# Turning h by DMA instead of by TensorE in a fused cross-attention and expert kernel

## The chip, the cores and the metric

The kernel runs on one core of a Trainium2 chip. The metric is the device time of one execution in microseconds. The kernel before took 281.07 us (median of three runs, 281.0 to 282.23). All times in the text are microseconds.

## The reference, cut to what matters

`x` is 4 x 512 x 512 (2048 rows of 512), float32. Two stages follow each other:

```
h   = layernorm(x)                                   # per row
e   = expert of the row's token id                   # 4 experts, ctx[e] is 512 x 512
out = (silu(h @ ctx[e].T) * (h @ ctx[e].T)) @ ctx[e].T   # down projection by the same matrix
x1  = x + tanh(g_xattn) * out
h2  = layernorm(x1); per batch: gate on mean(h2), the best 2 of 6 experts
y   = sum of the two experts' gelu(h2 @ W1 + b1) @ W2 + b2, weighted
res = x1 + tanh(g_ffn) * y
```

In the first stage the gate and the up projection are one product, so a tile takes two products of 512 x 512.

## The kernel before, in words

The rows are sorted by expert into 19 tiles of 128 rows (`TILES`), padded where an expert's rows end. A tile j goes through this: GpSimd (POOL) gathers its rows from `x` by an indirect DMA into one of 7 places of `x_ring` (`gather`, L502); VectorE (DVE) takes mean and variance (`rows_statistics`, L661); POOL raises variance + eps to the power -1/2 (`inverse_root`, L506); DVE writes the normalised rows into the one buffer `h` (`normalise`, L683); TensorE (PE) turns `h` by four 128 x 128 transposes (`transpose_h`, L1189); ScalarE (ACT) rounds the turned tile into `hT_hi` (`h_high`, L960) and DVE takes the rest as `hT_lo` (`h_low`, L689). PE then makes the first product from twelve matmuls of 512 columns (hi x hi, hi x lo, lo x hi: `first_product`, L1235). ACT takes silu (`silu_of`), DVE multiplies (`up`, L702) into the one buffer `a`, PE turns `a` (`transpose_a`, L1196), ACT rounds it (`a_high`, L965), DVE takes the rest (`a_low`, L696), and PE makes the second product, twelve matmuls again. DVE adds it to the rows in the ring (`add`, L668) and takes their statistics (`statistics`, L673). POOL raises that variance too and scatters the rows to DRAM by an indirect DMA (`scatter`, L511); `landed(j)` (L518) waits until this scatter has landed, after which a gather may overwrite that place of the ring.

The work of each engine is written out by hand, in order, and each engine runs its list in order; semaphores stand between them. In step j of the steady part (j from 5) PE does `transpose_a(j-1)`, `transpose_h(j+1)`, `first_product(j)`, `second_product(j-1)`. DVE does `add(j-2)` and `a_low(j-1)` (in either order), `rows_statistics(j+2)`, `statistics(j-2)`, `up(j)`, `normalise(j+2)`, `h_low(j+1)`. ACT does `a_high(j-1)`, `silu_of(j)`, `h_high(j+1)`. POOL's loop over j (L555) does `inverse_root(j+4)`, `scatter(j)`, `landed(j-1)`, `gather(j+6)`; so its turn j falls into PE's step j+2. Steps 12 to 18 (`PREP` on) carry work for the second stage besides: DVE normalises `x1` of the first batch in steps 12 and 13, PE turns it in step 14 (`transpose_first_h2`), ACT rounds it there (`ffn_h_high(0)`, L1019), and PE makes the gate's logits at the head of step 15 (`logits`, L1346), which wait for that rounding; ACT's `exponents(0)` with two table loads follows in step 15. SyncE (SP) loads `x1` of the first batch once seven tiles have landed, and the experts' weights once the gate has chosen.

In the second stage a batch has a first half (s = 0) and a second (s = 1), each with three blocks of hidden columns, gelu, and output. Weights are parted into hi (`split_high`, ACT, L1051) and lo (`split_low`, `split_low_last`, DVE). For batches 2 and 3 (`by_dma`, L188) the turn of `h2` is already done by DMA: ACT parts each float32 into two 16-bit words (`part_words`, L1029), SP issues `dma_start_transpose` (`turn_words`, L450), ACT joins the words again (`join_words`, L1038).

Of the kernel before, what the change touches and what calls it, by code (L numbers as in the profile page):

```python
# [33 lines left out]
P = 128  # L34
# [41 lines left out]
def flamingo_kernel(nc, x, ids, ctx, g_xattn, g_ffn, gate_w, w1, b1, w2, b2, out):  # L76
# [19 lines left out]
    PAIRED = range(E + 1, TILES)  # L96
    LATER = TILES - E
    BY_ACT = (0, 1)
    BY_DVE = tuple(n for n in range(E * KD) if n not in BY_ACT)
# [18 lines left out]
    with ExitStack() as stack:  # L118
# [15 lines left out]
        h = sb("h", [P, D])  # L134
        hT_hi = sb("hT_hi", [P, KD, P], FP32R)
        hT_lo = sb("hT_lo", [P, KD, P], FP32R)
        a = sb("a", [P, F1])
# [29 lines left out]
        hT1_lo = nc.alloc_sbuf_tensor_at("hT1_lo", [P, KD, P], FP32R, offset=w_lo1 + KD * P * 4)  # L167

        def hT_of(j):
            return (hT1_hi, hT1_lo) if j == 1 else (hT_hi, hT_lo)  # L170

# [177 lines left out]
        b1_padded, masks_made = sem("b1_padded"), sem("masks_made")  # L349
        half_copied, folded = sem("half_copied"), sem("folded")  # L350
        words_made, words_joined = sem("words_made"), sem("words_joined")
        words_turned = [sem(f"words_turned{t}") for t in range(TT)]
# [35 lines left out]
        def _(sp):  # L388
# [51 lines left out]
            def store(b):  # L440
                for t in range(TT):
                    store_rows(sp, b, t, halves_of(b, t)[0], TT * b + t + 1)

            sp.wait_ge(ctxT_done, E * KD)
            sp.wait_ge(tiles_landed, EARLY)
            load_x1(0)
            sp.wait_ge(rows_done, 1)
            sp.wait_ge(pads_made, 2)
# [27 lines left out]
        def _(pool):  # L476
# [77 lines left out]
            gather(E + 2, E + 2)  # L554
            for j in range(1, TILES):  # L555
                paired = j + 2 in PAIRED or j + 3 in PAIRED
                if paired and j + AHEAD < TILES:
                    inverse_root(j + AHEAD)
                scatter(j, j % RING)
                if not paired and j + AHEAD < TILES:  # L560
                    inverse_root(j + AHEAD)
                landed(j - 1)
                if j + RING - 1 < TILES:
                    gather(j + RING - 1, (j - 1) % RING)
            landed(TILES - 1)


        @block.vector
        def _(dve):
# [113 lines left out]
            def normalise(j):  # L683
                dve.wait_ge(rstd_ready, j + 1)
                at_least(dve, hT_done, j)
                dve.tensor_scalar(h[:, :], ring_row(j, 0, D), mv1[:, 0:1], rstd1[:, :],
                                  ALU.subtract, ALU.mult).then_inc(h_ready, 1)

            def h_low(j):  # L689
                dve.wait_ge(hT_hi_done, j + 1)  # L690
                hi, lo = hT_of(j)
                dve.tensor_tensor(lo[:, :, :].rearrange("p k t -> p (k t)"), hT_bank(j)[:, :],
                                  hi[:, :, :].rearrange("p k t -> p (k t)").bitcast(FP32),
                                  ALU.subtract).then_inc(hT_lo_done, 1)
# [57 lines left out]
            rows_of(slice(E, TILES), o_ps[0], LATER, routed)  # L752
            ctx_low(15)
            for j in range(2, PREP):
                a_low(j - 1)
                if j in PAIRED or j + 1 in PAIRED:
                    if j not in PAIRED:
                        normalise(j + 1)
                    add(j - 2, y_ps)
                    rows_statistics(j + 2)  # L760
                    statistics(j - 2)
                    up(j)
                    normalise(j + 2)
                    h_low(j + 1)
                else:
                    if j > 2:
                        normalise(j + 1)
                        residual(j - 2)
                    h_low(j + 1)
                    up(j)  # L770
                    rows_statistics(j + 2)
# [44 lines left out]
            def split_low(b, s, piece):  # L816
                dve.wait_ge(hi_done[s], len(PARTS) * b + piece + 1)
                raw, hi, lo = w_raw[s], w_hi[s], w_lo[s]
                if s == 0 or piece == 0:
                    dve.tensor_tensor(part_of(lo, piece), part_of(raw, piece), part_of(hi, piece).bitcast(FP32),  # L820
                                      ALU.subtract).then_inc(lo_done[s], 1)
                elif piece == 1:

                    dve.tensor_tensor(rest_of(hi, P + LW, REST), rest_of(raw, P, P + LW), rest_of(hi, P, P + LW).bitcast(FP32),
                                      ALU.subtract)
                    dve.tensor_tensor(rest_of(lo, 0, P), rest_of(raw, 0, P), rest_of(hi, 0, P).bitcast(FP32),
                                      ALU.subtract).then_inc(lo_done[s], 1)
                else:
                    dve.tensor_tensor(lo[:, W1N:WN - D], raw[:, W1N:WN - D], hi[:, W1N:WN - D].bitcast(FP32),  # L829
                                      ALU.subtract).then_inc(lo_done[s], 1)  # L830
# [51 lines left out]
            for j in range(PREP, TILES):  # L882
                if j == PREP + 3:
                    scale_logits(0)
                add(j - 2, y_ps)
                a_low(j - 1)
                if j + 2 < TILES:
                    rows_statistics(j + 2)
                statistics(j - 2)
                up(j)  # L890
                if j + 2 < TILES:
                    normalise(j + 2)
                if j + 1 < TILES:
                    h_low(j + 1)
                if j < PREP + 2:
# [18 lines left out]

            def batch(b, more):
                weigh(b, 0, 0)
                weigh(b, 0, 1)
                split_low(b, 1, 0)
                split_low(b, 1, 1)
                weigh(b, 0, 2)  # L920
                if more and not by_dma(b + 1):
                    ffn_normalise(b + 1)
                if not by_dma(b + 1):
                    split_low_last(b)
                if more:
# [3 lines left out]
                    mixing(b + 1)  # L929
                if by_dma(b + 1):  # L930
                    split_low_last(b)
                split_low(b, 1, 2)
                weigh(b, 1, 0)
# [20 lines left out]
        def _(sc):  # L954
# [58 lines left out]
            for n in range(12, 16):  # L1013
                ctx_high(n)
            for j in range(2, PREP):
                a_high(j - 1)
                silu_of(j)
                h_high(j + 1)
            def ffn_h_high(b, banks):  # L1019
# [61 lines left out]
            for j in range(PREP, TILES):  # L1081
                a_high(j - 1)
                if j == TILES - 1:
                    split_high(0, 0, 2)
                silu_of(j)
                if j + 1 < TILES:
                    h_high(j + 1)
                if j == PREP + 2:
                    ffn_h_high(0, o_ps)
                if j == PREP + 3:  # L1090
                    exponents(0)
                    bring_tables(ACT.Silu)
                if j == PREP + 5:
                    split_high(0, 0, 0)
                    split_high(0, 0, 1)
# [4 lines left out]
            def batch(b, more):  # L1100

                bring_tables(ACT.Gelu)
                wait_apart(sc, gate_ready, b + 1, waited)
                chosen = [sc.value_load(top_idx[0:1, s:s + 1], min_val=0, max_val=NE - 1) for s in range(2)]
                gelu_of(b, 0, 0, chosen)
                split_high(b, 1, 0)
                split_high(b, 1, 1)
                if by_dma(b + 1):
                    join_words(b + 1, [0])
                gelu_of(b, 0, 1, chosen)  # L1110
                if by_dma(b + 1):
                    join_words(b + 1, [1, 2])
                else:
                    split_high(b, 1, 2)
                for c in range(2, FC):
                    gelu_of(b, 0, c, chosen)
                if by_dma(b + 1):
                    join_words(b + 1, [3])
                    sc.wait_ge(words_joined, TT * b)
                if more:  # L1120
                    ffn_h_high(b + 1, t_ps)
                    if by_dma(b + 1):
                        split_high(b, 1, 2)
                    bring_tables(ACT.Exp)
# [20 lines left out]
        def _(pe):  # L1145
# [164 lines left out]
            def tile_step(j):  # L1310
# [3 lines left out]
                transpose_a(j - 1)  # L1314
                if j in PAIRED:
                    transpose_h(j + 1)
# [29 lines left out]
            def logits(b):  # L1346
                if isinstance(b, int) and b == 0:
                    pe.wait_ge(h2T_hi_done, KD)
                    pe.wait_ge(hT_lo_done, PREP + 4)
                else:  # L1350
# [68 lines left out]
            for j in range(PREP, TILES):  # L1419
                if j == PREP + 3:  # L1420
                    logits(0)
                transpose_a(j - 1)
                if j == PREP + 3:
                    pe.wait_ge(neg_max_ready, 1)
                if j + 1 < TILES:
                    transpose_h(j + 1)
                first_product(j, e)
# [61 lines left out]
```

## Time and profile before

| | |
|---|---|
| runs | 281.07 median, 281.0 to 282.23 |
| the profiled execution, its own time | 281.05 |
| its span, first to last instruction | 279.2 |
| PE busy, share of the span | 97% |
| DVE, ACT, POOL busy | 77%, 48%, 25% |
| granted TensorE clock | full speed in all 40 slices |

The span is about 1.9 us shorter than the execution's own time; what lies around it is start and end of the program. The shares of busy time are averages over both stages. The row stage (19 tiles) lasts until about 142 us, the expert stage from there to the end. "L1211" is the line of `product` and stands for the row stage's matmuls; L1193 are the turns of `h`, L1202 those of `a`.

### The profile page before, as it was taken

The page shows a single profiled execution, that of the slowest core. Times are in us where ns is not written, and L with a number is a line of the kernel's source. Part 1 is how long each engine was busy: PE and PEld are TensorE (multiplying, and loading weights), DVE is VectorE, ACT ScalarE, POOL GpSimd, SP SyncE. Part 2 cuts the span into 40 slices and gives each one's busy share as a digit, 9 for nine tenths or more (in the row PEclk, how much of TensorE's full clock was granted, in tenths as well). Part 3 has the DMA queues.
Part 4 walks back from the last instruction along what each step waited for, and adds up shares of the span by engine and source line. Part 5 has one row for each costly group of instructions (what it writes and reads, how often), then busy time and mean ns, then how long its engine had stood idle before and what let it go on. Part 6 is the DMA issues. An engine that isn't in the chain of part 4 may idle for free.

```text
span 279.2 us, 4519 instructions
## 1 busy us (share of the span) xinstructions
PE 271.9 (97%) x1400; PEld 222.3 (80%) x1400; DVE 215.7 (77%) x500; ACT 133.7 (48%) x216; POOL 70.1 (25%) x113
## 2 busy tenths in 40 slices
PE   7999999999999999999999999999999999999995
PEld 6888888888888888888788877878768777788783
DVE  8798988877777888688996769975799649878074
ACT  4745322222222223462627185799576994634020
POOL 5565165555544555324133000000000000000000
PEclk9999999999999999999999999999999999999999
DMA  6870033222356322319702637994299504940004
GB/s 196 299 249 14 2 112 113 79 75 86 106 104 210 102 77 78 75 40 280 230 38 78 195 108 224 257 256 151 53 300 209 176 2 117 307 163 2 0 0 150
DMA packets 32610, 37.10 MB, mean 133 GB/s; under 512 B 12584, under 2 KB 21038, under 8 KB 32588
## 3 DMA queue, kind: packets, MB, share of 16 engines
q1 hardware_dynamic: 29376, 26.69, 32.8%
q0 software_dynamic: 3040, 9.98, 12.0%
q8 instruction: 12, 0.20, 0.3%
q10 hardware_dynamic: 172, 0.15, 0.2%
q14 instruction: 10, 0.08, 0.1%
HBM read 25.52 MB, written 9.19 MB: 124 GB/s over the span
## 4 chain that ended last, share of the span: by engine, by line
PE 75%; ACT 10%; DVE 7%; issue 3%; DMA 2%; POOL 0%; ACTq 0%; SPq 0%; DVEq 0%
PE bank L1211 38%; PE bank L1185 8%; PE bank L1187 8%; PE bank L1186 8%; PE bank L1193 3%; PE bank L1202 3%; ACT joined L1043 3%; DMA raw_ctx<-in_ctx 2%; ACT w_hi L1058 2%; PE bank L1263 2%; ACT ctx_hi L1026 1%; PE bank L1408 1%; PE bank L1409 1%; DVE x_even L879 1%; DVE w_lo L829 1%
## 5 line engine op out<-in xcount | busy, mean ns | idle before, releaser
L1185 PE MATMUL bank<-w_lo,ctx_hi 128*128 128x512 f32 x80 | 31.8, 397 | 0.1
L1187 PE MATMUL bank<-w_hi,ctx_lo 128*128 128x512 f32 x80 | 31.2, 391 | 0.0
L1186 PE MATMUL bank<-w_hi,ctx_hi 128*128 128x512 f32 x80 | 31.2, 390 | 0.0
L973 ACT ACTIVATE a<-bank 128x512 f32<-128x512 f32 x19 | 11.4, 599 | 40.5 <-PE bank L1211 40.5
L968 ACT ACTIVATE aT_hi<-bank 128x512 fp32r<-128x512 f32 x18 | 10.8, 598 | 33.9 <-PE bank L1202 33.9
L1058 ACT ACTIVATE w_hi<-w_raw 128x512 fp32r<-128x512 f32 (+3 forms) x24 | 23.7, 1019 | 1.4 <-DMA w_raw<-in_L_ffn_W 1.4
L1185 PE MATMUL bank<-ctx_lo,w_hi 128*128 128x512 f32 x60 | 23.6, 394 | 0.0
L1211 PE MATMUL bank<-ctx_hi,hT_hi 128*128 (+1 forms) x80 | 23.3, 414 | 0.1
L1186 PE MATMUL bank<-ctx_hi,w_hi 128*128 128x512 f32 x60 | 23.4, 390 | 0.0
L1187 PE MATMUL bank<-ctx_hi,w_lo 128*128 128x512 f32 x60 | 23.4, 390 | 0.0
L503 POOL DMA_INDIRECT x_ring<-in_x,get_rows x19 | 19.3, 1016 | 14.8 <-DVE put_rows L653 9.8
L1065 ACT ACTIVATE act<-bank,tables 128x512 f32<-128x512 f32 x16 | 11.0, 685 | 24.6 <-PE bank L1187 24.1
L1211 PE MATMUL bank<-ctx_hi,hT_lo 128*128 (+1 forms) x80 | 21.6, 392 | 0.0
L1211 PE MATMUL bank<-ctx_lo,hT_hi 128*128 (+1 forms) x80 | 21.5, 391 | 0.0
L515 POOL DMA_INDIRECT x_scratch<-x_ring,put_rows x19 | 20.1, 1056 | 5.4 <-POOL x_ring L514 5.4
L698 DVE TENSOR_TENSOR aT_lo<-bank,aT_hi 128x512 fp32r<-128x512 f32 x18 | 12.4, 688 | 10.4 <-ACT aT_hi L968 10.3
L1211 PE MATMUL bank<-ctx_hi,aT_hi 128*128 (+1 forms) x72 | 19.9, 398 | 0.0
L508 POOL TENSOR_TENSOR rstd<-ve,half 128x1 f32<-128x1 f32 x19 | 10.8, 571 | 36.1 <-DVE ve L666 36.1
L1211 PE MATMUL bank<-ctx_hi,aT_lo 128*128 (+1 forms) x72 | 19.6, 392 | 0.0
L1211 PE MATMUL bank<-ctx_lo,aT_hi 128*128 (+1 forms) x72 | 19.3, 390 | 0.0
L870 DVE TENSOR_SCALAR ctx_hi<-act,mix 128x512 fp32r<-128x512 f32 x16 | 7.7, 483 | 13.7 <-ACT act L1065 13.6
L1185 PEld LDWEIGHTS bank<-w_lo,ctx_hi 128*128 128x128 f32 x80 | 15.0, 188 | 4.0 <-issue 0.9
(221 smaller groups left out, 625.6 us busy)
## 6 DMA issues: line engine op xcount, KB each, us to landing
raw_ctx<-in_ctx SPq DMA_DIRECT2D x4, 1024.0 KB, 8.1
w_raw<-in_L_ffn_W SPq DMA_DIRECT2D x8, 512.0 KB, 4.9
x_even<-x_scratch SPq DMA_DIRECT2D x8, 257.0 KB, 3.8
w_raw<-in_L_ffn_W SPq DMA_DIRECT2D x8, 256.0 KB, 4.6
w_raw<-in_L_ffn_W SPq DMA_DIRECT2D x4, 448.0 KB, 3.6
out<-x_even SPq DMA_DIRECT2D x7, 256.0 KB, 2.4
w_raw<-in_L_ffn_W SPq DMA_DIRECT2D x4, 384.0 KB, 6.4
x_odd<-x_scratch SPq DMA_DIRECT2D x4, 257.0 KB, 3.4
```

The source lines that it names most:

```text
L503: pool.indirect_dma_start(x_ring[:, r * DS:r * DS + D], None, x_rows, bass.IndirectOffsetOnAxis(get_rows[:, j:j + 1], 0)).then_inc(gathere ...
L508: pool.tensor_tensor(rstd1[:, :], ve1[:, :], half[:, 0:1], ALU.pow).then_inc(rstd_ready, 1)
L515: pool.indirect_dma_start(x1_rows, bass.IndirectOffsetOnAxis(put_rows[:, j:j + 1], 0), x_ring[:, r * DS:(r + 1) * DS], None).then_inc(scat ...
L698: dve.tensor_tensor(lo[:, :, :].rearrange("p k t -> p (k t)"), bank[:, :], hi[:, :, :].rearrange("p k t -> p (k t)").bitcast(FP32), ALU.su ...
L968: sc.activation(aT_hi[:, :, :].rearrange("p k t -> p (k t)"), aT_ps[:, :], ACT.Copy).then_inc(aT_hi_done, 1)
L973: sc.activation(a[:, :], z_bank(j)[:, :], ACT.Silu).then_inc(silu_done, 1)
L1058: sc.activation(part_of(w_hi[s], piece, s), part_of(w_raw[s], piece, s), ACT.Copy).then_inc(hi_done[s], 1)
L1065: sc.activation(act[:, c % 2, :], hid_ps[k % 2][:, :], ACT.Gelu, bias=b1_of(s, c, slice(0, P), chosen[s])).then_inc(gelu_done, 1)
L1185: pe.matmul(dst, s_hi, m_lo, start=first, stop=False)
L1186: pe.matmul(dst, s_hi, m_hi, start=False, stop=False)
L1187: return pe.matmul(dst, s_lo, m_hi, start=False, stop=last)
L1211: return pe.matmul(dst[:, :], src[:, k, :], weights[:, bass.ds(e * (KD * F1) + k * F1, F1)], start=first, stop=last)
```

## The change

For tiles 7 to 18 (`TURNED` = 7) the turn of `h` leaves PE. After `normalise`, ACT parts `h` into 16-bit words (`part_row`), SP turns the 128 x 1024 words by one DMA transpose (`turn_row_words`), and ACT joins them (`join_row`) and rounds the joined tile into `hT_hi`; DVE's `h_low` reads the joined tile. Tiles of odd number get buffers of their own. In these steps `rows_statistics` and `normalise` run three tiles ahead instead of two, `normalise` waits until ACT has parted the tile before, and stands ahead of `up` in DVE's list; POOL's loop has from its third turn on the order `landed`, `gather`, `inverse_root`, `scatter`. SP's load of the first batch's `x1` stands behind the DMA transposes of tiles 7 to 13. In batches 1 and 2 of the expert stage the last piece of the second half's weights is split before the first gelu, and the joins are placed later. The diff, cut to its core:

```diff
@@ -166,8 +168,17 @@
+        row_words = nc.alloc_sbuf_tensor_at("row_words", [P, 2, 2, D], U16, offset=weights + 3 * WN * 4)
+        row_words_T = nc.alloc_sbuf_tensor_at("row_words_T", [P, 2, 2 * KD, P], U16, offset=weights + 3 * WN * 4 + 8 * D)
+        hT_joined = [nc.alloc_sbuf_tensor_at("hT_joined0", [P, KD * P], FP32, offset=hT_lo_at),
+                     nc.alloc_sbuf_tensor_at("hT_joined1", [P, KD * P], FP32, offset=w_lo1 + KD * P * 4)]
+        def turned(j):
+            return TURNED <= j < TILES
         def hT_of(j):
-            return (hT1_hi, hT1_lo) if j == 1 else (hT_hi, hT_lo)
+            return (hT1_hi, hT1_lo) if j == 1 or (turned(j) and j % 2) else (hT_hi, hT_lo)
...
@@ -441,9 +454,18 @@
+            def turn_row_words(js):
+                for j in js:
+                    sp.wait_ge(row_words_made, j - TURNED + 1)
+                    sp.dma_start_transpose(row_words_T[:, j % 2], row_words[:, j % 2].rearrange("p g d -> p (g d)")).then_inc(
+                        row_words_turned[j % 2], 16)
             sp.wait_ge(ctxT_done, E * KD)
+            turn_row_words(range(TURNED, EARLY + TURNED))
             sp.wait_ge(tiles_landed, EARLY)
             load_x1(0)
+            turn_row_words(range(EARLY + TURNED, TILES))
             sp.wait_ge(rows_done, 1)
...
@@ -552,16 +574,26 @@
             gather(E + 2, E + 2)
-            for j in range(1, TILES):
+            for j in range(1, TURNED - AHEAD):
                 paired = j + 2 in PAIRED or j + 3 in PAIRED
-                if paired and j + AHEAD < TILES:
+                if paired:
                     inverse_root(j + AHEAD)
                 scatter(j, j % RING)
-                if not paired and j + AHEAD < TILES:
+                if not paired:
                     inverse_root(j + AHEAD)
+                landed(j - 1)
+                gather(j + RING - 1, (j - 1) % RING)
+            for j in range(TURNED - AHEAD, TILES):
                 landed(j - 1)
                     gather(j + RING - 1, (j - 1) % RING)
+                if j == TURNED - AHEAD:
+                    inverse_root(j + AHEAD)
+                if j > TURNED - AHEAD and j + AHEAD + 1 < TILES:
+                    inverse_root(j + AHEAD + 1)
+                scatter(j, j % RING)
+                if j == TURNED - AHEAD:
+                    inverse_root(j + AHEAD + 1)
             landed(TILES - 1)
...
@@ -682,14 +714,16 @@
                 dve.wait_ge(rstd_ready, j + 1)
-                at_least(dve, hT_done, j)
+                at_least(dve, hT_done, min(j, TURNED))
+                at_least(dve, row_words_made, j - TURNED)
                 dve.tensor_scalar(h[:, :], ring_row(j, 0, D), mv1[:, 0:1], rstd1[:, :],
                 hi, lo = hT_of(j)
-                dve.tensor_tensor(lo[:, :, :].rearrange("p k t -> p (k t)"), hT_bank(j)[:, :],
+                source = hT_joined[j % 2] if turned(j) else hT_bank(j)
+                dve.tensor_tensor(lo[:, :, :].rearrange("p k t -> p (k t)"), source[:, :],
                                   hi[:, :, :].rearrange("p k t -> p (k t)").bitcast(FP32),
...
@@ -751,7 +785,23 @@
             ctx_low(15)
+            def row_step(j):
+                add(j - 2, y_ps)
+                a_low(j - 1)
+                if j + 3 < TILES:
+                    rows_statistics(j + 3)
+                statistics(j - 2)
+                if j + 3 < TILES:
+                    normalise(j + 3)
+                up(j)
+                if j + 1 < TILES:
+                    h_low(j + 1)
             for j in range(2, PREP):
+                if j >= TURNED - 1:
+                    row_step(j)
+                    continue
                 a_low(j - 1)
...
@@ -762,6 +812,9 @@
                     h_low(j + 1)
+                    if j == TURNED - 2:
+                        rows_statistics(j + 3)
+                        normalise(j + 3)
                 else:
...
@@ -882,16 +936,7 @@
                     scale_logits(0)
-                add(j - 2, y_ps)
-                a_low(j - 1)
-                if j + 2 < TILES:
-                    rows_statistics(j + 2)
-                statistics(j - 2)
-                up(j)
-                if j + 2 < TILES:
-                    normalise(j + 2)
-                if j + 1 < TILES:
-                    h_low(j + 1)
+                row_step(j)
                 if j < PREP + 2:
...
@@ -913,23 +958,27 @@
             def batch(b, more):
+                joined_ahead = by_dma(b + 1)
                 weigh(b, 0, 0)
                 split_low(b, 1, 1)
+                if joined_ahead:
+                    split_low_last(b)
                 weigh(b, 0, 2)
-                if more and not by_dma(b + 1):
-                    ffn_normalise(b + 1)
-                if not by_dma(b + 1):
+                if joined_ahead:
+                    split_low(b, 1, 2)
+                else:
+                    if more:
+                        ffn_normalise(b + 1)
                     split_low_last(b)
                     mixing(b + 1)
-                if by_dma(b + 1):
-                    split_low_last(b)
-                split_low(b, 1, 2)
+                if not joined_ahead:
+                    split_low(b, 1, 2)
                 weigh(b, 1, 0)
...
@@ -1012,10 +1061,37 @@
                 ctx_high(n)
+            def part_row(j):
+                sc.wait_ge(h_ready, j + 1)
+                at_least(sc, row_words_turned[j % 2], 16 * ((j - TURNED) // 2))
+                sc.activation(row_words[:, j % 2], h[:, :].bitcast(U16).rearrange("p (d g) -> p g d", g=2),
+                              ACT.Copy).then_inc(row_words_made, 1)
+            def join_row(j):
+                sc.wait_ge(row_words_turned[j % 2], 16 * ((j - TURNED) // 2 + 1))
+                sc.wait_ge(z_done, j - 1)
+                to = hT_joined[j % 2][:, :].bitcast(U16).rearrange("p (k s g) -> p g k s", k=KD, g=2)
+                sc.activation(to, row_words_T[:, j % 2].rearrange("p (g k) s -> p g k s", g=2), ACT.Copy).then_inc(row_words_joined, 1)
+                sc.wait_ge(row_words_joined, j - TURNED + 1)
+                sc.activation(hT_of(j)[0][:, :, :].rearrange("p k t -> p (k t)"), hT_joined[j % 2][:, :], ACT.Copy).then_inc(hT_hi_done, 1)
+            def tile_step(j):
+                a_high(j - 1)
+                if turned(j + 1):
+                    join_row(j + 1)
+                silu_of(j)
+                if j + 1 < TURNED:
+                    h_high(j + 1)
+                if j == TURNED - 2:
+                    part_row(TURNED)
+                if j >= TURNED - 2 and turned(j + 3):
+                    part_row(j + 3)
             for j in range(2, PREP):
-                a_high(j - 1)
-                silu_of(j)
-                h_high(j + 1)
+                tile_step(j)
             def ffn_h_high(b, banks):
...
@@ -1102,25 +1178,23 @@
                 chosen = [sc.value_load(top_idx[0:1, s:s + 1], min_val=0, max_val=NE - 1) for s in range(2)]
+                joined_ahead = by_dma(b + 1)
+                if joined_ahead:
+                    split_high(b, 1, 2)
                 gelu_of(b, 0, 0, chosen)
                 split_high(b, 1, 1)
-                if by_dma(b + 1):
-                    join_words(b + 1, [0])
                 gelu_of(b, 0, 1, chosen)
-                if by_dma(b + 1):
-                    join_words(b + 1, [1, 2])
+                if joined_ahead:
+                    join_words(b + 1, [0, 1])
                 else:
                     split_high(b, 1, 2)
-                for c in range(2, FC):
-                    gelu_of(b, 0, c, chosen)
-                if by_dma(b + 1):
-                    join_words(b + 1, [3])
+                gelu_of(b, 0, 2, chosen)
+                if joined_ahead:
+                    join_words(b + 1, [2, 3])
                     sc.wait_ge(words_joined, TT * b)
                     ffn_h_high(b + 1, t_ps)
-                    if by_dma(b + 1):
-                        split_high(b, 1, 2)
                     bring_tables(ACT.Exp)
...
@@ -1312,7 +1386,7 @@
                 transpose_a(j - 1)
-                if j in PAIRED:
+                if j in PAIRED and not turned(j + 1):
                     transpose_h(j + 1)
...
@@ -1346,7 +1420,7 @@
                     pe.wait_ge(h2T_hi_done, KD)
-                    pe.wait_ge(hT_lo_done, PREP + 4)
+                    pe.wait_ge(hT_lo_done, TURNED)
                 else:
...
@@ -1420,10 +1494,6 @@
                 transpose_a(j - 1)
-                if j == PREP + 3:
-                    pe.wait_ge(neg_max_ready, 1)
-                if j + 1 < TILES:
-                    transpose_h(j + 1)
                 first_product(j, e)
```

## Rows read from the trace of the kernel before

**Rows 1.** The page, part 1: busy us (share of the span) xinstructions of each engine.

```profile
PE 271.9 (97%) x1400; PEld 222.3 (80%) x1400; DVE 215.7 (77%) x500; ACT 133.7 (48%) x216; POOL 70.1 (25%) x113
```

**Rows 2.** Chain that ended last, in order of time: start us, us, what.

```profile
62.67 0.44 PE bank L1202 x4
...
88.07 0.44 PE bank L1202 x4
...
88.51 0.44 PE bank L1193 x4
...
107.13 0.44 PE bank L1202 x4
...
115.53 0.59 PE bank L1202 x4
...
135.01 0.44 PE bank L1202 x4
```

**Rows 3.** DVE, instructions in order of time: start, us, operation, idle before.

```profile
54.88 0.54 DVE L686 TENSOR_SCALAR h<-x_ring,mv,rstd 128x512 f32<-128x512 f32 x1
...
89.17 0.69 DVE L698 TENSOR_TENSOR aT_lo<-bank,aT_hi 128x512 fp32r<-128x512 f32 x1 [1.31 <-ACT aT_hi L968]
...
92.46 0.68 DVE L704 TENSOR_TENSOR a<-bank,a 128x512 f32<-128x512 f32 x1
...
93.51 0.68 DVE L692 TENSOR_TENSOR hT_lo<-bank,hT_hi 128x512 fp32r<-128x512 f32 x1
```

**Rows 4.** ACT, instructions in order of time, same columns.

```profile
88.54 0.60 ACT L968 ACTIVATE aT_hi<-bank 128x512 fp32r<-128x512 f32 x1 [2.08 <-PE bank L1202]
...
91.74 0.60 ACT L973 ACTIVATE a<-bank 128x512 f32<-128x512 f32 x1 [2.60 <-PE bank L1211]
...
120.52 1.28 ACT L1048 ACT_TABLE_LOAD   x1
...
123.51 0.20 ACT L979 ACTIVATE warm<-tg 1x2 f32<-1x2 f32 x1
```

**Rows 5.** POOL, instructions in order of time, same columns.

```profile
91.61 0.57 POOL L508 TENSOR_TENSOR rstd<-ve,half 128x1 f32<-128x1 f32 x1 [2.15 <-DVE ve L666]
...
92.62 0.55 POOL L514 TENSOR_TENSOR x_ring<-x_ring,half 128x1 f32<-128x1 f32 x1 [0.44 <-DVE x_ring L677]
...
93.46 1.07 POOL L515 DMA_INDIRECT x_scratch<-x_ring,put_rows  x1 [0.29 <-POOL x_ring L514]
...
94.83 0.97 POOL L503 DMA_INDIRECT x_ring<-in_x,get_rows  x1 [0.30 <-issue]
```

**Rows 6.** Scatters (L515), landing of all, of 55 to 108 us, of 140 to 148 us.

```profile
DMA to landing us min/median/max: 2.8/3.7/6.5
...
DMA to landing us min/median/max: 3.1/3.9/5.3
...
DMA to landing us min/median/max: 3.4/3.5/3.5
```

**Rows 7.** DMA transposes (L454), landing of all eight, us from issue.

```profile
DMA to landing us min/median/max: 3.1/4.1/5.6
```

**Rows 8.** Groups of instructions by form: xcount, busy us, mean ns.

```profile
L1043 ACT ACTIVATE joined<-words_T 128x1024 uint16<-128x1024 uint16 x8 | 10.6, 1362 | 0.0
...
L1035 ACT ACTIVATE words<-h 128x1024 uint16<-128x1024 uint16 x8 | 8.0, 1041 | 0.0
...
L1026 ACT ACTIVATE h2T_hi<-bank 128x512 fp32r<-128x512 f32 x4 | 2.3, 615 | 0.0
```

**Rows 9.** PE and ACT in the expert stage, in order of time.

```profile
207.18 0.47 PE L1408 MATMUL bank<-w_hi,ctx_hi 128*128 128x512 f32 x1 [0.49 <-DVE ctx_hi L858]
...
181.91 0.69 ACT L1065 ACTIVATE act<-bank,tables 128x512 f32<-128x512 f32 x1 [1.86 <-PE bank L1187]
...
193.34 0.63 ACT L1057 ACTIVATE w_lo<-b_rows 64x512 fp32r<-64x512 f32 x1
...
193.98 1.49 ACT L1058 ACTIVATE w_hi<-w_raw 128x1536 fp32r<-128x1536 f32 x1
```

More of the change, by code:

```diff
@@ L97, in flamingo_kernel @@
     LATER = TILES - E
+    TURNED = E + 3
     BY_ACT = (0, 1)
@@ L135, in flamingo_kernel @@
         hT_hi = sb("hT_hi", [P, KD, P], FP32R)
+        hT_lo_at = (nc.sbuf_base + 31) // 32 * 32
         hT_lo = sb("hT_lo", [P, KD, P], FP32R)
@@ L350, in flamingo_kernel @@
         half_copied, folded = sem("half_copied"), sem("folded")
+        row_words_made, row_words_joined = sem("row_words_made"), sem("row_words_joined")
+        row_words_turned = [sem(f"row_words_turned{i}") for i in range(2)]
         words_made, words_joined = sem("words_made"), sem("words_joined")
@@ L816, in split_low @@
             def split_low(b, s, piece):
-                dve.wait_ge(hi_done[s], len(PARTS) * b + piece + 1)
+                place = (1, 2, 0)[piece] if s == 1 and by_dma(b + 1) else piece
+                dve.wait_ge(hi_done[s], len(PARTS) * b + place + 1)
                 raw, hi, lo = w_raw[s], w_hi[s], w_lo[s]
@@ L1081, in _ @@
             for j in range(PREP, TILES):
-                a_high(j - 1)
                 if j == TILES - 1:
+                    a_high(j - 1)
                     split_high(0, 0, 2)
-                silu_of(j)
-                if j + 1 < TILES:
-                    h_high(j + 1)
+                    silu_of(j)
+                else:
+                    tile_step(j)
                 if j == PREP + 2:
@@ L1422, in _ @@
                 transpose_a(j - 1)
-                if j == PREP + 3:
-                    pe.wait_ge(neg_max_ready, 1)
-                if j + 1 < TILES:
-                    transpose_h(j + 1)
                 first_product(j, e)
```

## The prediction

> **What bounds the kernel now.** I read the page's busy shares first: PE 97%, DVE 77%, ACT 48%, POOL 25% [rows 1]. Then the chain that ended last, in order of time. In the row stage it is PE alone: a turn of a (0.44), a turn of h (0.44), 24 matmuls, and again. I call S_j the start of `transpose_a(j-1)` in step j. From S_11 = 88.07 to S_14 = 107.13 a step takes 6.35 [rows 2]. The timelines of the other engines inside one step show who could follow a faster PE. DVE works from 89.17 to 94.19, 5.0 of the 6.35, and sat idle before for 1.31 [rows 3]. ACT rounds a at S+0.47 and makes silu at S+3.67 [rows 4]; it has two thirds of the step free. POOL has its root, its power for the scatter, the scatter, the gather [rows 5], and nothing in the step before waits for it. So PE bounds the row stage, and turns of h taken from PE are worth 0.44 each if all others keep pace: 12 x 0.44 = 5.3. A step would be 5.91.
>
> **POOL's new order (the deciding term).** Before, turn j of POOL's loop is root, scatter(j), then `landed(j-1)`, whose scatter was issued a whole step earlier, then gather: no wait. After, it is `landed(j-1)`, gather(j+6), root(j+5), scatter(j). Now the scatter that POOL waits for is the one it issued last, and the root that DVE needs in this very step stands behind it. Behind the root wait `normalise(j+3)` and, in DVE's list, `up(j)`, and so PE's next turn of a. This is a ring within POOL. Its length, from end of root to end of root: power 0.55, gap 0.29, scatter issued to landed L, gap 0.30, gather 0.97, root 0.57 [rows 5], and twice 0.05 that I estimate between its instructions: 2.78 + L. L isn't on a row of the new order. Bounds: 2.8, the lowest of all 19, and 3.9, the median of the nine steady ones, which have a gather issued close behind [rows 6]; below by nothing more, above 5.3, one that met the load of x1. I take 3.45, from the two scatters with no indirect transfer behind them (3.4 and 3.5): in the new order the next gather is issued only after the landing, and the last one has its packets out before. The ring is then 6.23, against PE's 5.91 and 6.35 before. DVE isn't the limit: its 5.0 of work has the same instructions in another order.
>
> The Trainium skill, page "DMA: Bandwidth & Descriptors", section "Anatomy of one DMA — SWDGE (gpsimd) path", puts a DMA issued by GpSimd at about 2.0 plus its bytes over 436 GB/s. For 263 KB that is an estimate of 2.6, below each of the 19 landings here, and the ring would be 5.4, shorter than PE's step. The page adds that the receipt of a write to HBM can be slow, and a scatter writes to HBM. Its formula is the first rival below; the sum doesn't use it.
>
> **The way in (tiles 7 and 8).** `normalise(7)` ends at 55.42 [rows 3]. `part_row` costs 1.04 [rows 8], the DMA transpose 4.1 (3.1 to 5.6) [rows 7]: landed at 60.7. The join 1.36 [rows 8], rounding 0.60, silu(6) 0.60 behind it in ACT's list, `up(6)` 0.68: PE can begin step 7 at 64.1 instead of 62.67 [rows 2]. At the same time POOL's root(8) stands behind scatter(3), ends at 57.7 and lets `normalise(8)` end at 58.3, `part_row(8)` at 59.4; `a_high(5)` is queued behind it and ends at 60.0. From there a_low 0.65, two statistics 2 x 1.05: 62.75; power, gap, scatter issued at 63.65, landed 67.1, gap, gather, root: POOL's root in step 7 ends at N_7 = 69.0. From a root's end to PE's next step I count 0.08, normalise 0.45 (start to next start), up 0.68 and 0.06 = 1.27. S_8 = 70.3.
>
> **Steps 8 to 15.** Seven turns of the ring: N_14 = 69.0 + 7 x 6.23 = 112.6. Step 14 brings `ffn_h_high(0)`, which now stands behind `part_row(17)` in ACT's list, and that waits for `normalise(17)`: 112.6 + 0.62 + 1.1 = 114.3, then four roundings, 2.3 [rows 8], 116.7; the logits, which wait for them, 0.28: S_15 = 117.0 against 115.53 [rows 2], 1.5 late.
>
> **Steps 15 to 18.** POOL's turns have no gather now and are off the path. ACT in step 15: `normalise(18)` ends at S+4.3, part_row at S+5.35, the exponents with two table loads 3.2 (120.52 to 123.71 [rows 4]), `a_high(15)` at S+9.2, join and rounding 2.06, silu 0.6, up 0.7: S_17 = S_15 + 12.65 where PE alone gives 11.82. S_18 = S_15 + 18.55 = 135.55. Before it was 135.01. The row stage is **0.55 longer**: the 5.3 of removed turns are paid back by 1.5 on the way in, by the ring (7 x 0.32), by the logits' wait and by ACT's exponents. The gate's choice comes some 2 later, which the weights' loads can bear, as their split stands behind silu(17).
>
> **What costs nothing.** SP's DMA transposes: from `part_row(j+3)` to `join_row(j+3)` lie over 6, the landing is 4.1, at most 5.6 [rows 7]; if that cover went, each microsecond over would delay silu. Moving x1's load behind them: it lands about 97, wanted at 100; behind it nothing on SP is due before the gate. `h_low` from SBUF instead of PSUM: the same 0.68.
>
> **The expert stage's order.** Before, PE waits 0.49 for a DVE result at 207.18, and once more a batch later [rows 9]. The moved splits free DVE earlier, so both can go: -1.0. But ACT's split of the second half's last piece (0.63 + 1.49) now stands ahead of the first gelu, at 181.91 before [rows 9]. It needs weights and bias rows whose issue ended at 176.5; by the landings of the DMA transposes of the same stretch [rows 7] they are there at 179.6 to 182.1. ACT is free at 180.1, so the gelu comes at 182.2 to 184.3. PE's third hidden block asks for it at 184.3, its end 0.66 later: 0 to 0.6 lost, and the second gelu with its weighing, behind two more splits, 0 to 0.9. For two batches -1.0 to +0.8. I take +0.3, nearer the late end, since these rows are queued last behind the weights.
>
> **Sum.** 281.05 (the profiled execution's own time: span 279.2 and 1.9 around it) + 0.55 + 0.3 = 281.9; the median of the runs, 281.07, is the same. By 0.5%, 1.4, a measurement can tell this kernel from no change: 281.9 lies 0.3% above.
>
> **Rivals.**
> 1. *The ring is short.* If L is 2.8, as in one scatter of 19, the ring is 5.58 and PE's 5.91 binds. S_14 = 70.3 + 6 x 5.91 = 105.75, S_15 = that + 8.40 - 0.44 = 113.7, S_18 = 132.25, 2.75 earlier; with 0.3: **278.6**. It counts as faster from a ring of 5.91, L = 3.13; some steady scatters were at 3.1 [rows 6]. That the median of these is 3.9 speaks against.
> 2. *The ring is long.* One mechanism on the slow side: the landing of the scatter with a DMA transpose and a gather about it. At L = 3.9 the ring is 6.68, 7 x 0.45 = 3.15 more: **285.1**. It decides from L = 3.53 on (0.08 per turn). For it: a DMA transpose per step is new traffic. Against: by my times its packets come after the scatter's.
> 3. *All is hidden,* way in included: -5.3 and -1.0, **274.8**. Needs POOL and ACT both off the path.
> 4. *The change doesn't do what it says in the expert stage:* the row stage as forecast, but the early split costs its full 0.8: 282.4.
>
> **Chances.** Forecast (279.7 to 283.3) with rival 4: 0.45; rival 1: 0.24; rival 2: 0.26; rival 3: 0.05. Of the forecast's 0.45 about 0.31 lies within 0.5%, 0.12 above, 0.02 below. Faster 0.31, same 0.31, slower 0.38. The likeliest case's own range is 280.2 to 283.3; the range from rival 1 to rival 2 with the expert stage's bounds is 277.8 to 285.1.
>
> **What would show it.** Steps 8 to 14 of PE at 6.2, not 5.9, with PE idle before L1202 for DVE's a; `normalise` (L686's successor) waiting for POOL's root; POOL waiting for landings of its own scatters, near 3.45. S_7 at 64.1. PE waiting before the logits. Steps of 5.9 throughout would prove the ring wrong; steps over 6.5 rival 2. In the expert stage the waits at L1408 gone, and new ones of under 1 before the third hidden block and the first output of batches 1 and 2. Wrong altogether if DVE, not POOL, is what `up` waits behind.

## The result: 5% slower

The changed kernel took 295.19 (median of four runs, 293.75 to 297.27); the kernel before, beside it, 281.5 (281.0 to 282.23). The ratio is 1.0495, 95% interval 1.0466 to 1.0524. The forecast was 281.9, at most 285.1. The profiled execution of the changed kernel is its slowest run, 297.27, with a span of 295.5. Ratios in this text are taken over runs within 1.5% of the fastest of their kernel, which leaves out two of the ten runs of the last experiment and none of the others.

The page of the kernel after, part 1 (busy us and share of the span), the row of granted clock in 40 slices, and two groups of part 5:

```profile
PE 274.5 (93%) x1352; PEld 220.6 (75%) x1352; DVE 217.1 (73%) x500; ACT 162.9 (55%) x240; POOL 73.3 (25%) x113
...
PEclk9999999999979999979999979999999999999999
...
L525 POOL DMA_INDIRECT x_ring<-in_x,get_rows x19 | 18.8, 991 | 44.9 <-DMA x_scratch<-x_ring,put_rows 33.4
...
L719 DVE TENSOR_SCALAR h<-x_ring,mv,rstd 128x512 f32<-128x512 f32 x19 | 10.5, 551 | 15.2 <-POOL rstd L530 14.9
```

PE's share fell from 97% [rows 1] to 93%, with 48 turns fewer. POOL is busy 25% as before, yet its gathers now wait 33.4 for landings of scatters, and DVE's `normalise` waits 14.9 for POOL's root. A low busy share didn't mean that POOL was off the path.

The chain that ended last, in order of time, kernel after, three turns of POOL's ring (start us, us, what):

```profile
71.80 4.88 DMA x_scratch<-x_ring,put_rows
76.72 0.77 issue
77.49 0.98 POOL x_ring L525
78.48 0.58 POOL rstd L530
79.06 0.63 POOL x_ring L536
79.69 0.28 issue
79.96 3.65 DMA x_scratch<-x_ring,put_rows
83.65 0.77 issue
84.42 0.98 POOL x_ring L525
85.41 0.59 POOL rstd L530
86.00 0.62 POOL x_ring L536
86.62 0.28 issue
86.90 3.52 DMA x_scratch<-x_ring,put_rows
...
120.24 0.59 POOL rstd L530
```

Where the chain of before is PE alone [rows 2], this one has no PE from 63 to 121. It is scatter, landing, gather, root, power, scatter. In the timeline of PE (start, busy, operation, idle before), the heads of two steps of the kernel after:

```profile
72.14 0.66 PE L1276 MATMUL bank<-ident,a 128*128 128x128 f32 x4 [2.14 <-DVE a L738]
80.30 0.66 PE L1276 MATMUL bank<-ident,a 128*128 128x128 f32 x4 [2.04 <-DVE a L738]
```

Later in the same chain, the end of the row stage's scatters and the load of the second batch's rows:

```profile
138.23 7.63 DMA x_scratch<-x_ring,put_rows
...
148.09 3.16 DMA x_scratch<-x_ring,put_rows
...
161.90 3.98 DMA x_scratch<-x_ring,put_rows
...
167.29 5.00 DMA x_odd<-x_scratch
172.32 0.56 DVE h L831
172.93 1.33 PE bank L1407 x8
```

Starts of PE's steps, from the chains and timelines of PE, and the difference:

| | before | after | later by | eight places in the ring (below) |
|---|---|---|---|---|
| step 7 | 62.67 | 63.88 | 1.2 | 63.77 |
| step 14 | 107.13 | 115.22 | 8.1 | 105.30 |
| step 15 | 115.53 | 125.13 | 9.6 | 113.50 |
| step 18 | 135.01 | 144.72 | 9.7 | 132.14 |
| logits of the second batch | 164.38 | 179.18 | 14.8 | 161.69 |
| logits of the fourth batch | 228.57 | 245.57 | 17.0 | 225.69 |
| span | 279.2 | 295.5 | 16.3 | 275.6 |

8.1 comes by step 14, 1.5 with the logits' wait in step 14, 0.1 in steps 15 to 17, 5.1 with the second batch's rows, 2.2 in batches 1 and 2, and 0.7 comes back behind them. In steps 15 to 17 three removed turns should have gained 1.3; why they didn't is told below, at the granted clock.

### The profile page after: what moved, and what is told of

It reads as the page before. It is cut to its first block, busy times and chain, and to the rows that moved or that the text cites. A ratio compares the mean times of both kernels' runs of the same rounds, so it can differ in the third digit from the quotient of the medians.

```text
span 295.5 us, 4457 instructions
## 1 busy us (share of the span) xinstructions
PE 274.5 (93%) x1352; PEld 220.6 (75%) x1352; DVE 217.1 (73%) x500; ACT 162.9 (55%) x240; POOL 73.3 (25%) x113
## 4 chain that ended last, share of the span: by engine, by line
PE 39%; DMA 25%; POOL 8%; issue 7%; ACT 7%; DVE 6%; SPq 6%; ACTq 0%; DVEq 0%; POOLq 0%
DMA x_scratch<-x_ring,put_rows 19%; PE bank L1285 9%; PE bank L1259 7%; PE bank L1261 6%; PE bank L1260 6%; DMA b_rows<-in_L_ffn_b 4%; POOL x_ring L536 3%; POOL x_ring L525 3%; PE bank L1337 3%; POOL rstd L530 2%; ACT w_hi L1134 2%; DMA x_odd<-x_scratch 2%; PE bank L1227 1%; SPq L451 1%; PE bank L1276 1%
## 5 line engine op out<-in xcount | busy, mean ns | idle before, releaser
L525 POOL DMA_INDIRECT x_ring<-in_x,get_rows x19 | 18.8, 991 | 44.9 <-DMA x_scratch<-x_ring,put_rows 33.4
L1068 ACT ACTIVATE row_words<-h 128x1024 uint16<-128x1024 uint16 x12 | 12.7, 1057 | 21.7 <-DVE h L719 21.7
L1285 PE MATMUL bank<-ctx_hi,hT_hi 128*128 (+1 forms) x80 | 24.2, 426 | 0.3 <-ACT hT_hi L1012 0.3
L1285 PE MATMUL bank<-ctx_lo,hT_hi 128*128 (+1 forms) x80 | 23.3, 415 | 0.0
L537 POOL DMA_INDIRECT x_scratch<-x_ring,put_rows x19 | 21.4, 1127 | 5.4 <-POOL x_ring L536 5.4
L1285 PE MATMUL bank<-ctx_hi,hT_lo 128*128 (+1 forms) x80 | 22.5, 404 | 0.0
L719 DVE TENSOR_SCALAR h<-x_ring,mv,rstd 128x512 f32<-128x512 f32 x19 | 10.5, 551 | 15.2 <-POOL rstd L530 14.9
L874 DVE TENSOR_TENSOR w_lo<-w_raw,w_hi 128x512 fp32r<-128x512 f32 (+2 forms) x16 | 17.1, 1086 | 3.2 <-ACT w_hi L1134 3.1
```

Of the source, the lines that this page charges most:

```text
L525: pool.indirect_dma_start(x_ring[:, r * DS:r * DS + D], None, x_rows, bass.IndirectOffsetOnAxis(get_rows[:, j:j + 1], 0)).then_inc(gathere ...
L537: pool.indirect_dma_start(x1_rows, bass.IndirectOffsetOnAxis(put_rows[:, j:j + 1], 0), x_ring[:, r * DS:(r + 1) * DS], None).then_inc(scat ...
L1068: sc.activation(row_words[:, j % 2], h[:, :].bitcast(U16).rearrange("p (d g) -> p g d", g=2), ACT.Copy).then_inc(row_words_made, 1)
L1285: return pe.matmul(dst[:, :], src[:, k, :], weights[:, bass.ds(e * (KD * F1) + k * F1, F1)], start=first, stop=last)
```

## The experiments

Theory A: POOL's ring (its wait for the scatter that it issued last) sets the step, and the same order makes the last scatters a file that delays the second batch's rows. Rival B: the DMA transposes' traffic slows every landing. Rival C: ACT's parting and joining stand in the way. Rival D came later: that what a larger ring gains has nothing to do with the turns taken from PE.

### Eight places in the ring

```diff
-    RING = 7
+    RING = 8
 ...
-                landed(j - 1)
-                if j + RING - 1 < TILES:
-                    gather(j + RING - 1, (j - 1) % RING)
+                landed(j - 2)
+                if j + RING - 2 < TILES:
+                    gather(j + RING - 2, (j - 2) % RING)
```

The eighth place lies in memory that the expert stage uses later; the edit also has POOL wait for the turned `ctx`, and ACT for the landings, before either side uses that memory.

> The kernel after with one more place in the ring of rows (8 instead of 7, the eighth in memory that the expert stage uses later): gather(j+6) and the wait in front of it now stand for scatter(j-2), issued a whole step earlier, instead of scatter(j-1). Everything else is the kernel after: DMA transposes, three tiles ahead, POOL's order, the expert stage's order. Theory A (POOL's wait for its own last scatter sets the step, and what follows from it downstream): no wait of POOL's gathers for a landing in steps 8 to 14, PE's step 5.9 to 6.0 instead of about 7.2, step 15 begins near 114 instead of 125, and the whole takes 278 to 282. Rival B (the DMA transposes' traffic, some 12,700 more packets, slows the landings and with them everything): the step stays above 6.6 and the time above 288. Rival C (ACT's parting and joining stand too long ahead of silu and the rounding of a): steps above 6.3 with PE waiting for ACT, 284 to 290.

Measured: 277.87 (277.35 to 278.49), ratio to before 0.9884, interval 0.9861 to 0.9908. The turns of DMA and the order of DVE, ACT and POOL are those of the kernel after; only the wait is for a landing one step older. PE's steps in its timeline:

```profile
69.76 0.60 PE L1287 MATMUL bank<-ident,a 128*128 128x128 f32 x4
75.69 0.60 PE L1287 MATMUL bank<-ident,a 128*128 128x128 f32 x4
```

5.93 a step, without idle time before. Its waits (us in total, times, longest), and the landings of its scatters from 55 to 120 us:

```profile
POOL x_ring L531 <- DMA x_scratch<-x_ring,put_rows: 0.9, 1, 0.9
...
DVE h L728 <- POOL rstd L536: 0.7, 1, 0.7
```

```profile
DMA to landing us min/median/max: 4.9/5.1/5.3
```

Of the 33.4 that POOL's gathers waited, 0.9 is left. Rival B had a true part: landings are longer here than before, 5.1 against 4.0 in the same stretch, with a DMA transpose and a gather about each. But a landing that nobody waits for costs nothing. C and B fall as causes of the 5%: against the kernel after, 17.3 are gone, 9.9 of them by step 14.

### POOL's order alone, in the kernel before

```diff
-            for j in range(1, TILES):
+            for j in range(1, 3):
 ...
+            for j in range(3, TILES):
                 landed(j - 1)
                 if j + RING - 1 < TILES:
                     gather(j + RING - 1, (j - 1) % RING)
+                if j + AHEAD < TILES:
+                    inverse_root(j + AHEAD)
+                scatter(j, j % RING)
```

> The kernel before with one edit: POOL's loop has from its third turn on the order landed(j-1), gather(j+6), inverse_root(j+4), scatter(j). TensorE turns h as before, two tiles ahead, no DMA transposes. Theory A: POOL's ring of power, scatter, landing, gather and root comes to about 6.7 to 7.0 against PE's 6.35; the root that normalise(j+2) waits for comes late, steps grow by 0.3 to 0.6, and the load of the second batch's rows behind the last landing comes late besides: 284 to 290. Rival B: without DMA transposes the order costs nothing, 281 to 282.

Measured: 289.5 (287.92 to 291.2), ratio 1.0272, interval 1.0235 to 1.0308. No DMA transpose runs in its row stage, and the chain shows the same ring:

```profile
90.12 0.58 POOL rstd L508
90.70 0.62 POOL x_ring L514
91.60 4.76 DMA x_scratch<-x_ring,put_rows
96.41 0.77 issue
97.17 0.97 POOL x_ring L503
98.17 0.58 POOL rstd L508
```

From the root's end at 63.03 to that at 105.74 are six turns, 7.1 each. The kernel after has (120.83 - 70.90) / 7 = 7.1. The landings in these turns are 3.8 on the mean here and 3.85 there. The ring has the same length with and without DMA transposes: B is refuted for the ring.

### The same order with eight places

The last kernel with the ring's edit of the first experiment on top.

> The kernel before with POOL's new order and eight places in the ring: TensorE turns h, two tiles ahead, but POOL's wait is for a scatter issued a step earlier. Against the kernel with POOL's order alone (289.5) only the ring differs. Theory A: POOL is off the path again, PE's step is 6.35, and the time is that of the kernel before, 280.5 to 282. If the eight places gained anything by themselves (rival D: the gain of the kernel with DMA transposes and eight places comes from the ring and not from the turns taken from PE), it would be below 280, near 278.

Measured: 280.95 (280.7 to 281.77), ratio 0.9999, interval 0.9989 to 1.001. The order costs 8.5 with seven places and nothing with eight. The larger ring gains nothing of itself (rival D falls), so the gain of the first experiment against before comes with the rest of the change.

### The tail

```diff
             for j in range(TURNED - AHEAD, TILES):
-                landed(j - 1)
+                if j < TILES - 5:
+                    landed(j - 1)
 ...
                 scatter(j, j % RING)
+                if j >= TILES - 5:
+                    landed(j - 1)
```

> The kernel after with one edit: in POOL's turns 14 to 18, which gather nothing, scatter(j) stands before landed(j-1) again. The ring of turns 3 to 13 stays, so step 15 begins at 125 as in the kernel after. What goes is the file of scatters that wait for one another; the second batch's rows are then loaded at about 159 instead of 166, before PE wants them turned, and its wait of 3.3 with the stretch at half the clock behind it is gone. Theory A with its two parts (ring, then late load): 289 to 292 against 295.2. Rival: the load is bound by something else, no change (294 to 296).

Measured: 289.13 (286.97 to 290.21), ratio to before 1.0309, interval 1.0286 to 1.0333, 6.1 less than the kernel after. All five runs lie below all four of the kernel after. PE's wait of 3.28 before the second batch's turns isn't in its trace. The ring is left as it was, yet in the profiled execution, the fastest (286.97), step 15 begins at 122.6 and not at 125.1, and step 18 at 141.2 and not at 144.7: single landings and the granted clock vary between two executions. The other 6.8 by which the two spans differ come behind step 18. So the medians' 6.1 is the price of the tail only as nearly as such variation lets one say. The one order cost in two places: of the 17.3 between seven and eight places 9.9 stand at step 14, and about 6 come through its last five turns.

### The expert stage's order by itself, twice

The edit is the change's part in batches 1 and 2, put into the kernel before, and taken out of the kernel with eight places.

> The kernel before with only the new order of the expert stage in batches 1 and 2 (early split of the second half's last piece, later joins). In the kernel after, PE waits there 0.85 and 0.33 per batch before the third hidden block and the first output, where before it waited 0.49 and 0.2 per batch. So 0.5 to 1.2 slower than before: 281.6 to 282.3. The forecast had put -1.0 to +0.8 on it. If instead the waits in the kernel after come only from its late row stage, this kernel is 0.5 to 1.0 faster than before.

Measured: 281.0 (ten runs, 279.52 to 282.04), ratio 0.9992, interval 0.9973 to 1.0011. No difference in the runs, so neither of the two expectations.

> The kernel with eight places in the ring, with the expert stage's order of the kernel before. Row stage as in that kernel; if the expert order costs 0.5 to 1.2, this one is that much faster than it: 277 to 281. If it is the slower of the two, the new expert order is a gain once the row stage is in time.

Measured: 279.11 (278.91 to 279.58), ratio to before 0.9927, interval 0.9909 to 0.9945; with the new order 277.87. Here the new order is worth 1.2 and no loss. In the kernel after, PE did wait for it, as the forecast had it for a late split (timeline of PE, batch 1):

```profile
200.19 0.50 PE L1259 MATMUL bank<-ctx_lo,w_hi 128*128 128x512 f32 x1 [0.85 <-ACT act L1141]
...
203.53 0.47 PE L1259 MATMUL bank<-w_lo,ctx_hi 128*128 128x512 f32 x1 [0.33 <-DVE ctx_lo L925]
```

With eight places only the second of these is left (0.35 and 0.28 in the two batches); with the kernel before's row stage both are there, 0.17 and 0.33 in batch 1. The traces show more than the medians. From the start of the second batch's logits to the end of the span it is 114.8 in the kernel before and 113.7 with the new order (in its fastest run, the profiled one), 114.9 and 113.9 in the two kernels with eight places, one execution each. So in the traces the new order gains about 1.0 behind either row stage. Only behind the late row stage of the kernel after it is 116.3. Why ten runs of the first kernel, spread over 2.5, don't show the gain in their median stays open.

### The way in

On top of the kernel with eight places, ACT's list of steps 5 and 6 in another order:

```diff
                 a_high(j - 1)
+                if j == TURNED - 1:
+                    part_row(TURNED + 1)
+                    silu_of(j)
+                    join_row(j + 1)
+                    part_row(j + 3)
+                    return
```

> The kernel with DMA transposes and eight places, and in ACT's list of steps 5 and 6 the order a_high(5), part_row(8), silu(6), join_row(7), part_row(9) instead of part_row(8), a_high(5), join_row(7), silu(6), part_row(9). Step 6 took 7.6 there, of which 1.7 is loss: a_high(5) queued behind the parting, silu(6) behind the join that waits for the first DMA transpose. Step 6 should be 5.9 to 6.3 and the whole 1.3 to 1.7 less than 277.9: 276.2 to 276.6.

Measured: 276.26 (275.82 to 276.57), ratio to before 0.9823, interval 0.9804 to 0.9842. Step 6 in PE's timeline, 6.6 instead of 7.6:

```profile
56.05 0.60 PE L1293 MATMUL bank<-ident,a 128*128 128x128 f32 x4
...
62.64 0.66 PE L1293 MATMUL bank<-ident,a 128*128 128x128 f32 x4 [0.47 <-DVE a L747]
```

1.0 of the expected 1.3 to 1.7 within the step, 1.6 over the whole. This is the fastest kernel of the study, 1.8% under the kernel before.

### The last tile's parting later, too

```diff
+                if j == TILES - 2:      # silu_of(j), then join_row(j + 1)
 ...
+                if j == TILES - 3:
+                    part_row(TILES - 1)
```

> As the one with the way in reordered, and besides the last tile's parting moved from step 15 (where the exponents with two table loads follow) to step 16, and its join behind silu(17). Step 16 took 6.68 with ACT late at a_high(15) and silu(16); it should be 5.95 to 6.2: another 0.4 to 0.8 less, 275.5 to 276.1. If the late join of the last tile makes PE wait at step 18, nothing is gained.

Measured: 282.27 (ten runs, 279.49 to 285.46; 281.98 for the eight within 1.5% of the fastest), ratio 1.002, interval 0.9987 to 1.0054: 5.7 slower than without this edit by those eight. Step 16 did fall to 5.93 (119.58 to 125.51), but PE then waits in step 18:

```profile
138.40 1.19 PE L1308 MATMUL bank<-ctx_hi,aT_hi 128*128 x2 [3.29 <-DVE x_ring L712]
```

Neither expectation named the cause. SP's list has the last DMA transpose ahead of the experts' weights; the parting moved from 117.3 to 123.8, and SP issues the first weights at 128.6 instead of 122.7. ACT's split of them waited 3.17, DVE's low parts behind it, and DVE's `add` behind those. The forecast's sentence "behind it nothing on SP is due before the gate" was true, and here the gate was already open.

## Why the prediction was wrong, by its own steps

- **What bounds before, and 5.91 for PE's step: right.** With eight places it is 5.93.
- **POOL's ring: the mechanism right, the size wrong.** This is the step that failed: "The ring is then 6.23". It measures 7.13 from root to root, in two terms. *L*, taken as 3.45 from two scatters of 140 to 148 us, is 3.85 on the mean of the seven in these turns (3.34 to 4.88): 0.40 more. The steady ones' median of 3.9 [rows 6], which I had put on the rival's side, was the better guess, and the last scatter of all (148.81), which that window left out, took 4.1 with no indirect transfer behind it. And the gap between landing and gather, taken as 0.30 from a gather that waited for nothing [rows 5], is 0.81, of which the chain has 0.77 as "issue": 0.51 more. Over seven turns 0.90 each make 6.3. The ring's first turn adds 1.9: the root in step 7, N_7, ends at 70.9 for 69.0, with a landing of 4.60, the same gap and a scatter issued 0.3 later. So N_14 is 8.2 late, 120.83 for 112.6. Step 14 follows N_13 by 1.2 and begins at 115.2 where 107.7 was forecast.
- **Steps 15 to 17: right relative to the ring.** Step 15 begins 4.3 after N_14, where 4.4 was worked out. With eight places step 17 begins 12.66 and step 18 18.64 after step 15, for a forecast 12.65 and 18.55; in the kernel after a stretch at the lower clock is added.
- **"POOL's turns have no gather now and are off the path": wrong.** The steps didn't wait for them, but the scatters did for each other: 137.38 to 165.88, the last landing 15 after the last turn of a, where before the gap was 12. The longest landing among them, 7.63, fell into the load of the experts' weights (issued from 135.9 on), as two of 6.5 and 6.2 did before. The load of the second batch's rows stands behind the last landing. I had not followed what waits for a landing but the ring. The run with the tail put back prices it at about 6.
- **Granted clock: not in the forecast.** Three times the clock fell to the lower of its two levels, 1.2 GHz, for some microseconds: from 81, from 125.5 and from 173, behind waits of PE of 2.04, 1.73 and 3.28. Windows of the kernel after (us; busy us of PE, PEld, DVE, ACT, POOL with counts; PEclk; DMA share; GB/s):

```profile
125.00:130.00 5.00, 5.00 (x25) 4.02 (x22) 4.03 (x11) 2.47 (x3) 1.32 (x2) 0.66 0.10 18
...
172.00:176.00 4.00, 3.07 (x13) 2.68 (x14) 3.43 (x6) 1.38 (x4) 0.00 (x0) 0.70 0.63 207
```

  Step 15 took 7.57 where the same step took 5.98 with eight places at full clock: 1.6. It is a second price that such a wait can have, but not each has it: behind the wait of 2.14 before step 8 the clock stayed full. The stretch from 81 made step 9 take 7.57, too; the ring, which was longer than PE's step, took up most of that. The Trainium skill's page "TensorE: Matmul & The Clock Gate", section "Part 1: The HAM clock gate", has TensorE at 1.2 GHz after idling and at 2.4 GHz when busy; the trace agrees, with a mean of 0.66 in the five microseconds behind the logits' wait, though the wait of 2.14 shows that idling of that length isn't always followed by it.
- **The way in: nearly right,** 63.88 for a forecast 64.1, and the cause, ACT's list, shown by the run that reorders it.
- **The expert stage: the sign wrong behind a row stage in time, the waits right behind a late one.** Forecast +0.3 in -1.0 to +0.8. By the runs the two pairs give 0 and -1.2, by their traces (one execution each) -1.1 and -1.0, the lower end of the range. Inside the kernel after PE waited 1.2 per batch, at the two places that were forecast, and the stage is 1.5 longer than before, outside the range. ACT's early split waits for the bias rows in each kernel with the new order; it begins 18.3 and 19.2 after the logits of its batch in the kernel after, 17.1 and 18.0 with eight places. Why they land later there isn't shown.
- **The rivals.** Rival 1 gave 105.75, 113.7 and 132.25 for steps 14, 15 and 18 if the ring were shorter than PE's step. Eight places in the ring make that case: 105.30, 113.50, 132.14. Rival 2 had the direction, a long ring, at 7.13 and not its 6.68, and with the tail behind it. Its mechanism, a DMA transpose about the scatter, wasn't the cause: POOL's order alone gives 7.1 without any. My bounds moved the landing alone and left the gap at its lowest.
- **The Trainium skill's formula** ("DMA: Bandwidth & Descriptors", "Anatomy of one DMA — SWDGE (gpsimd) path") would have made the ring 5.4. No scatter of any run landed within its 2.6; the shortest took 2.8. Whether the receipt of the write is what takes longer, as the Trainium skill warns in the same section, no run here shows.

## What to carry to other kernels

An engine that is busy 25% can set the time once its list contains a wait for its own last transfer: add up the whole ring, landing and wake-up included, and compare it with the step of the engine that bounds. When work is brought a step further ahead, the ring of buffers has to grow with it; one more place turned 5% slower into 1.2% faster here. For each moved transfer or wait, follow everything queued behind it on its queue, down to loads of a later stage.

## What the runs showed of the hardware that was not expected

- A gather whose engine had waited for a landing started 0.81 after it (0.77 of this is "issue" in the chain) in every turn of the ring, in two kernels; between a scatter and a gather that waited for nothing the gap was 0.30. The wake-up alone doesn't explain it: in the last turns of the kernel after, a power on the same engine, behind the same kind of wait and the same counting of tiles, started 0.18 after the landing (157.53 + 3.34 = 160.87). The other 0.63 goes with the start of a gather behind a wait; what it consists of isn't shown. From the chain of the kernel after:

```profile
157.53 3.34 DMA x_scratch<-x_ring,put_rows
161.05 0.57 POOL x_ring L536
```

- A scatter of 128 rows of 2 KB landed after 5.1 (median) with a DMA transpose and a gather about it, 4.0 with a gather alone, and 3.8 to 3.85 (mean of the turns in the chain, single ones 3.0 to 4.9) when the next gather waited for it.
- The clock fell to half behind six of the seven waits of PE of 1.7 to 3.3 in these traces (2.04, 1.73 and 3.28 in the kernel after, 2.20, 2.27 and 3.29 in others; not 2.14).
